# Attention over a masked graph on one core: 16 late key tiles instead of 12, their blocks moved by DMA alone and per query tile, and a new order on TensorE

## The reference, cut to what matters

```python
h = relu(layernorm(x))                         # x: 4096 x 256
adj = max(adjacency, eye)                      # 4096 x 4096
q, k, v = h @ Wq[hd], h @ Wk[hd], h @ Wv[hd]   # 8 heads, 64 wide
scores = q @ k.T * 64**-0.5 + 0.01*eye - 1e16*(1 - adj)
out = x + sum_hd(softmax(scores) @ v @ Wo[hd])
```

## Time and profile before

| | |
|---|---|
| three timed executions | 3120.87, 3127.58, 3130.91 us |
| profiled execution, span | 3131.2 us; no time of its own is listed apart from that span |
| granted TensorE clock, mean | 0.992 |
| TensorE busy | 3056.8 us (98%), 18368 matmuls |
| VectorE busy | 2444.3 us (78%) |
| ScalarE busy | 2171.6 us (69%) |
| GpSimd busy | 492.8 us (16%) |
| mean DMA rate | 86 GB/s |

### The profile page before, as it was taken

The page is one execution under the profiler, slowest core; times in us unless marked ns, Lnnn a source line. Parts: engine busy times, 40 slices in busy tenths (PEclk is TensorE's granted clock), DMA queues, the critical chain, the costliest instruction groups (busy, mean ns, idle before and its releaser), DMA issues.

```text
span 3131.2 us, 58791 instructions
## 1 busy us (share of the span) xinstructions
PE 3056.8 (98%) x18368; PEld 1892.8 (60%) x18368; DVE 2444.3 (78%) x4345; ACT 2171.6 (69%) x3297; POOL 492.8 (16%) x658
## 2 busy tenths in 40 slices
PE   7999999999999999999989999999999999999998
PEld 5566666666666666666556655666665666565664
DVE  6778788887878887887557877878877778777775
ACT  3677777777777777777547767767777667677675
POOL 3011111101111110111001111111111111111110
PEclk9999999999999999999999999999999999999999
DMA  5234444433444443344424433444433444433442
GB/s 154 53 85 88 95 79 98 84 81 78 91 91 84 94 85 85 73 95 87 94 74 80 88 84 73 87 93 81 93 79 72 86 94 81 93 79 72 89 93 52
DMA packets 217847, 267.82 MB, mean 86 GB/s; under 512 B 57472, under 2 KB 176768, under 8 KB 217728
## 3 DMA queue, kind: packets, MB, share of 16 engines
q1 hardware_dynamic: 173568, 178.51, 24.6%
q0 software_dynamic: 41984, 83.91, 16.1%
q10 hardware_dynamic: 2176, 4.19, 0.4%
HBM read 169.87 MB, written 12.71 MB: 58 GB/s over the span
## 4 chain that ended last, share of the span: by engine, by line
PE 92%; DVE 3%; issue 3%; DMA 1%; SPq 1%; DVEq 0%; ACT 0%; POOL 0%; POOLq 0%
PE psS L383 31%; PE psO L406 23%; PE psT L396 21%; PE psO L417 10%; PE psP L368 2%; PE psS L341 2%; DVE S L631 1%; PE psP L426 1%; PE psO L356 1%; PE psP L356 1%; DVE PT L645 1%; DMA S<-in_x 1%; SPq L239 0%; DMA S<-hT_scratch 0%; PE psT L327 0%
## 5 line engine op out<-in xcount | busy, mean ns | idle before, releaser
L631 DVE CUSTOM_DVE_ANT_0 S<-psS,B 128x1024 f32<-128x1024 f32 x1024 | 1239.6, 1211 | 169.0 <-PE psS L383 151.5
L517 ACT ACTIVATE S<-S,negm 128x1536 f32<-128x1536 f32 (+1 forms) x768 | 1094.8, 1427 | 62.9 <-DVE negm L638 59.7
L524 ACT ACTIVATE PT<-psT 128x512 f32<-128x512 f32 x768 | 457.0, 595 | 656.0 <-PE psT L396 654.3
L406 PE MATMUL psO<-PT,V 128*64 128x256 f32 x5120 | 836.0, 405 | 0.0
L396 PE MATMUL psT<-ident,S 128*128 128x128 f32 x5120 | 797.6, 283 | 31.4 <-DVE PT L645 24.3
L396 PEld LDWEIGHTS psT<-ident,S 128*128 128x128 f32 x5120 | 566.2, 141 | 398.2 <-issue 293.6
L383 PE MATMUL psS<-K,QH 128*128 128x512 f32 x2048 | 738.3, 442 | 8.4 <-DVE mx L631 5.9
L383 PE MATMUL psS<-K,QL 128*128 128x512 f32 x2048 | 643.8, 395 | 0.0
L645 DVE COPY PT<-psT 128x512 f32<-128x512 f32 x512 | 352.7, 689 | 332.4 <-PE psT L396 292.1
L658 DVE STREAM_TRANSPOSE S<-S 128x1536 f32<-128x1536 f32 x256 | 454.0, 1773 | 38.0 <-PE psO L417 37.9
L406 PEld LDWEIGHTS psO<-PT,V 128*64 128x64 f32 x5120 | 254.1, 135 | 362.4 <-issue 248.6
(11 more groups left out here) (52 smaller groups left out, 1056.1 us busy)
## 6 DMA issues: line engine op xcount, KB each, us to landing
S<-S SPq DMA_DIRECT2D x1536, 96.0 KB, 2.2
B<-in_adj POOLq DMA_DIRECT2D x256, 256.0 KB, 5.4
hq<-hT_scratch SPq DMA_DIRECT2D x32, 256.0 KB, 3.2
RB<-rden_scratch SPq DMA_DIRECT2D x128, 64.0 KB, 3.2
S<-in_x SPq DMA_DIRECT2D x8, 512.0 KB, 3.6
hT_scratch<-S ACTq DMA_DIRECT2D x8, 512.0 KB, 4.1
acc<-in_x POOLq DMA_DIRECT2D x16, 256.0 KB, 4.5
partial_scratch<-res POOLq DMA_DIRECT2D x16, 256.0 KB, 3.2
```

Of the source, the lines that this page charges most:

```text
L406: last = nc.tensor.matmul(psO[a * KD:(a + 1) * KD, 0:QW], V[:, 2 * s + a, h * KD:(h + 1) * KD], PT[:, s % RING, a * QW:(a + 1) * QW], star ...
L517: nc.scalar.activation(part, part, ACT.Exp, bias=negm[:, h % 2, q:q + 1], accum_out=sums[:, h % 2, q, e:e + 1]).then_inc(probs_ready, 1)
L524: nc.scalar.activation(PT[:, s % RING, :], psT[s % 2][:, :], ACT.Copy).then_inc(pt_act, 1)
L631: nc.vector.tensor_tensor_reduce(out=part, in0=psS[j % 2][:, :], in1=B[:, q, k * SLOT:(k + 1) * SLOT], scale=SCALE, scalar=LOWEST, op0=ALU ...
```

## The change

- `LATE` goes from 12 to 16, so TensorE transposes 16 key tiles in 8 slots instead of 20 in 10, and `values_late` has 16 tiles instead of 12. `T1` now covers the whole row of query tile 1 of the step before.
- All 16 pieces of a query tile are moved by DMA, one DMA for each piece and query tile, with a semaphore for each query tile: 32 DMAs a step on the SP queue instead of 12. `copy_late` is gone.
- ScalarE takes every transposed slot; VectorE's `take_slot` is gone.
- TensorE's step is four periods (`PERIODS`) of two transposed slots and two score slots; the late values stand in two halves, one in the third period and one behind the fourth, and slots 4 to 7 of the values at the end.
- On VectorE the order of the masks, of the sum of halves and of `add_heads` changes.

```diff
-LATE = 12
+LATE = 16
-MOVES = QUAD * (QUAD - 1)
+MOVES = QUAD * QUAD
...
-            sp.wait_ge(late_transposed, count(i, h, QT, QT))
-            for qi in range(QUAD):
-                for qj in range(QUAD):
-                    if qi != qj:
-                        src, dst = late_blocks(h, qi, qj)
-                        sp.dma_start(dst, src).then_inc(late_moved, 16)
+            for q in range(QT):
+                sp.wait_ge(late_transposed, count(i, h, QT, q + 1))
+                for qi in range(QUAD):
+                    for qj in range(QUAD):
+                        src, dst = late_blocks(h, q, qi, qj)
+                        sp.dma_start(dst, src).then_inc(late_moved[q], 16)
...
+        def values_late(i, h, tiles):
+            if tiles[0] == 0:
+                for q in range(QT):
+                    pe.wait_ge(late_moved[q], count(i, h, 16 * MOVES, 16 * MOVES))
...
+            for c in range(PERIODS):
+                for e in range(2):
+                    transposes(i, h, 2 * c + e)
+                    pair_scores(i, h, c, nxt, nxt2, e)
+                if c == 0 and nxt2 and h % 2 == 0:
+                    query(i2, h2, h2 == 0, isinstance(i, int) and i == 0 and h == 0)
+                if c == 1:
+                    values(i, h, 0)
+                    values(i, h, 1)
+                if c == 2:
+                    values(i, h, 2)
+                    values(i, h, 3)
+                    values_late(i, h, range(LATE_FIRST))
+                if c == 3 and prev and h % 2 == 0:
+                    if nxt2:
+                        pe.wait_ge(q_lo, count(i2, h2, 1, 2))
+                    project(*last_step(i, h))
+            values_late(i, h, range(LATE_FIRST, LATE))
+            for s in range(4, TS):
+                values(i, h, s)
...
+            if nxt:
+                mask(i1, h1, 6)
+                mask(i1, h1, 7)
+            if nxt2:
+                mask(i2, h2, 0)
+            if nxt:
+                transpose_late(i1, h1, 0, True)
+            if nxt2:
+                mask(i2, h2, 1)
+            if nxt:
+                transpose_late(i1, h1, 1, True)
```

More of the change, by code:

```diff
@@ L153, in wait_taken @@
     def wait_taken(engine, i, h, s):
-        slots, taken, start = (ACT_SLOTS, pt_act, PT_START) if s % TS in ACT_SLOTS else (DVE_SLOTS, pt_dve, 0)
-        engine.wait_ge(taken, count(i, h, len(slots), slots.index(s % TS) + 1 + start - (len(slots) if s < 0 else 0)))
+        engine.wait_ge(pt_act, count(i, h, TS, s + 1 + PT_START))
     def T1(h):
@@ L347, in keys_values @@
                 pe.wait_ge(wqo_in, 16 * (DC + 2))
-                query(0, 0, True, True)
+                query(0, 0, True, True, first=True)
             for u, read in ((0, v_act), (1, v_dve)):
@@ L358, in keys_values, with query @@
                 last.then_inc(v_proj, 1)
-        def query(i, h, wait_hq, first):
+        def query(i, h, wait_hq, free, first=False):
             if wait_hq:
@@ L427, in project, with pair_scores, step @@
             last.then_inc(projected, 2)
-        def step(i, h, nxt, nxt2, prev):
+        def pair_scores(i, h, c, nxt, nxt2, e):
             i1, h1 = (i, h + 1) if h + 1 < GROUP else (i + 1, 0)
             i2, h2 = (i, h + 2) if h + 2 < GROUP else (i + 1, h + 2 - GROUP)
-            for c in range(SUBSTEPS):
-                transposes(i, h, 2 * c)
+            j = 2 * c + 2 + e
+            if j < SLOTS:
                 if nxt:
-                    scores(i1, h1, c + 2)
-                if prev and h % 2 == 0 and c == PROJECT_AT:
-                    pe.wait_ge(q_lo, count(i, h, 1, 2))
-                    project(*last_step(i, h))
[L439 to L454, removed]
+                    scores(i1, h1, j)
+            elif nxt2:
+                scores(i2, h2, j - SLOTS)
+        def step(i, h, nxt, nxt2, prev):
+            i2, h2 = (i, h + 2) if h + 2 < GROUP else (i + 1, h + 2 - GROUP)
+            for c in range(PERIODS):
[14 more added lines that the diff above has]
+                        pe.wait_ge(q_lo, count(i2, h2, 1, 2))
+                    project(*last_step(i, h))
+            values_late(i, h, range(LATE_FIRST, LATE))
+            for s in range(4, TS):
+                values(i, h, s)
         pe.sem_inc(v_proj, START)
@@ L625, in mask @@
                 dve.wait_ge(bias_ready, i * QT + (q + 1))
-            if j == SPT + 1 and not first:
-                dve.wait_ge(late_moved, count(i, h, 16 * MOVES, 0))
-                dve.wait_ge(late_copied, count(i, h, QUAD, 0))
+            if not first:
+                for tq in range(QT):
+                    if j == t1_first_slot(tq):
+                        dve.wait_ge(late_moved[tq], count(i, h, 16 * MOVES, 0))
             wait_apart(dve, scores_ready, count(i, h, SLOTS, j + 1), dve_passed)
@@ L692, in step @@
             i2, h2 = (i, h + 2) if h + 2 < GROUP else (i + 1, h + 2 - GROUP)
[L693 to L700, removed]
-                    denominators(i, h)
-                if nxt2 and h % 2 == 0 and c > QUERY_AT:
-                    query_lo(i2, h2, c - QUERY_AT - 1)
-            if nxt:
-                mask(i1, h1, SLOTS - 2)
-                mask(i1, h1, SLOTS - 1)
-                transpose_late(i1, h1, 0, True)
+            if nxt:
+                mask(i1, h1, 2)
+                mask(i1, h1, 3)
+            if prev:
+                sum_halves(*last_step(i, h))
+            if nxt:
+                mask(i1, h1, 4)
+            if nxt2 and h % 2 == 0:
+                query_lo(i2, h2, 0)
+                query_lo(i2, h2, 1)
+            if nxt:
+                mask(i1, h1, 5)
+            denominators(i, h)
+            if h % 2 and not (isinstance(i, int) and i == 0 and h == 1):
+                add_heads(*((i, 1) if h == 3 else (i - 1, 3)))
+            if nxt:
+                mask(i1, h1, 6)
+                mask(i1, h1, 7)
             if nxt2:
```

91 lines of the change are left out of this document (42 added, 49 removed).

## The result

The changed kernel takes **4212.98 us** (median of 4 runs, 4207.15 to 4216.27), the kernel before 3127.8 us: a ratio of 1.347, 95% interval 1.345 to 1.349. The forecast was 3650 us in a range of 3010 to 4100: the direction was right, half of the slowdown was foreseen (522 us of 1085), and the measured time lies over the range's upper end.

The account below looks back on a forecast made before the run. The prediction took a ring through SP's 32 moves to bound the changed kernel: 10.3 + 16.5 = 26.8 us a step, 4.1 over before, 520 us more over 128 steps, so 3650 us. The range was 3010 to 4100 us.

Parts of the forecast that it names:

- the ring: Late values, TensorE's scores, mask, late transpose, SP's 32 moves, next late values: 10.3 + 31 c, 26.8 us a step.
- TensorE's own 20.2 us a step: TensorE's work in the new order, against 22.74 us; were that all, 325 us would be won.
- The issue interval c: Time from one late move's issue to the next on SP, taken as 0.53 us; break-even at 0.40.
- lower bound of 0.37: Lowest c on SP: denominators' store, 0.33 us, plus 0.04 between moves; gives a 21.8 us step and 3010 us.
- upper bound: Highest c on SP, about 0.64 us from the old two-row moves; gives a 30.3 us step and 4100 us.
- rival 2: SP's issue time doesn't change with the move's form: c 0.64 to 0.65, 4100 us; chance 0.27.
- three terms on TensorE: In the ring: late matmuls and change 1.89 us, transposed slot 0.41, score slot's start to its mask 1.38.
- busy share of about 75%: Expected sign in the profile after: TensorE's busy share falls from 98% to about 75%.
- The second ring: Not in the prediction: masks of slots 4 and 6 overwrite the block the moves read, so wait for the moves.
- VectorE and ScalarE at nothing: Both engines' changed work was costed at nothing while the step is longer than about 20 us.
- The landing: Last move's issue to landing, mean 2.7 us, plus 0.22 us for the semaphore to reach TensorE.
- The 50 ns: Skill's dispatch time for each DMA; with c near 0.1 the ring would be nowhere near TensorE.

Follow-up runs that it names:

- run 1: Changed kernel with half of the moves left out, 16 a step instead of 32, late probabilities wrong: 2811.14 us, ratio 0.899 to the kernel before.
- run 5: Changed kernel with the late transpose of query tile 0 ahead of the first mask of the step after next on VectorE: 4089.3 us, ratio 1.309.
- run 6: Changed kernel with the 16 moves of query tile 1 issued from ScalarE's queue, those of tile 0 from SP: 3654.87 us, ratio 1.168.
- run 4: Changed kernel with unread filler matmuls on TensorE, ten ahead of slot 6 and twelve ahead of the late values: 4130.51 us, ratio 1.320.
- run 2: Changed kernel with the first half of the late values moved from the third period to the end of the step: 4002.76 us, ratio 1.280.
- run 7: Kernel before with only its moves split by query tile, 24 one-row DMAs a step instead of 12 two-row ones: 3241.91 us, ratio 1.037.
- run 3: Changed kernel with both query tiles of a piece in one DMA, 16 two-row moves a step instead of 32: 4089.09 us, ratio 1.308.
- run 9: Changed kernel with 8 moves of a query tile by DMA, 4 pieces copied by ScalarE and 4 by GpSimd: 2938.63 us, ratio 0.940.

## Why the prediction was wrong in size

- **What bounds, and the ring.** Right. The chain of waits went from TensorE to SP's issues, and TensorE's late values wait for the moves once a step. Runs 1, 5 and 6 confirm it with numbers (1402 us for sixteen issues, 0.97 us for a 0.9 us earlier start, 558 us for a second queue).
- **TensorE's own 20.2 us a step.** Right as a floor: run 1 gained 317 us of the 325, with a step of 20.4 us. The step of before was read from one pair, 22.74 us; by the first move of each step over the whole trace it is 23.05, with 181 us outside the steps and not 220. The forecast total hardly feels it, since it adds the difference of steps to the whole.
- **The issue interval c. This is the step that failed first.** I took 0.53 from a single issue of the nearest form, the denominators' load. Measured: 0.63 from start to start (32 in 20.15 us), with 0.51 for the first move behind a pause, 0.59 in the median and 0.04 between. That is 3.2 us a step of the 4.6 that were missing (26.8 forecast, 31.4 measured), some 410 us. The trace of before had the warning. The same store of the denominators takes 0.33 us at 248.48, after a pause, but there is also this row of the same timeline of SP, right behind moves that end at 271.81:

```profile
271.86 0.58 SPq L241 DMA_DIRECT2D rden_scratch<-rden  x1
```

So the lower bound of 0.37 was none either. That row is no accident: in the trace of before seven stores begin within 0.1 us of the move ahead of them, 0.59 us in the median, and the 36 behind more than 1 us of pause take 0.33. For the store and for the move of one row an issue alone and an issue behind others are two prices (the move of two rows has 0.60 us for both); for 32 in a row only the second holds, and the twelve moves of before were the one row that showed it. That they stood as the upper bound (rival 2) gave 4100 us, 110 short.
- **The clock.** Not in the sum at all. All terms on TensorE were taken at full clock, though the prediction itself said that TensorE would wait 6 us a step. The three terms on TensorE are 1.5 us over the forecast ones in the mean of the turns (1.57 in the one shown); run 4 gets 0.64 us of a step back by filling part of the waits, so that much is shown for the clock by an experiment, and the rest by the granted clock beside the longer terms. This is what puts the time over the range: with c at its upper bound the sum was 30.3 us, and 31.4 were measured with an interval no longer than that bound. The busy share of about 75% came true (76%) by luck: the step is 4.6 us longer than forecast, and the matmuls are longer at the lower clock. Run 1 has the same matmuls busy for 2677.6 us, which would be 64% of this span.
- **The second ring.** Missed. I followed the semaphore of the moves to TensorE and not to the masks, which wait for it too, though the diff showed both. It didn't change this time much, since both rings have nearly the same length, but run 2 shows that it was decisive for any repair: the obvious one, late values at the end, gives 210 us instead of 800. The prediction also put all of TensorE's waiting at the late values; 3.5 us a step stand there, and 4.2 ahead of score slots, for masks.
- **VectorE and ScalarE at nothing.** Right: 53% and 44% busy.
- **The landing.** 2.7 us and 0.2 to reach TensorE: near enough in the mean (3.08 us from the last move's start to the late values, 2.9 forecast). It varies from 2.1 to 6.0 us.
- **The 50 ns that the prediction cites.** The Trainium skill, page "DMA: Bandwidth & Descriptors", section "Anatomy of one DMA — SWDGE (gpsimd) path", has about 50 ns of dispatch and a small, variable time for the descriptors. That section is on DMAs issued by GpSimd, and the moves here are issued by SP and ScalarE, so it was no measure for them: they take 0.51 to 0.61 us an issue, in every form tried. By the same page's section "Rules for kernel authors" DMAs spread over several engines only save the issuing engine's time. Run 6 agrees on what is saved, and here just that was worth 558 us.

## What to carry to other kernels

Count a DMA queue like an engine: number of issues by the interval between issues back to back, read from a row in which several follow each other, never from a lone one. Then follow each semaphore of the changed part to all who wait for it, and for each look whether what it does leads back to the next issue; a queue that is half idle on the average sets the pace as soon as it lies in such a ring. And a sum that makes TensorE wait some microseconds has to price what it does next at the lower clock.

## What the runs showed of the hardware that was not expected

- One issue on SP takes 0.59 to 0.60 us whether it carries one row of 2048 bytes a partition, one of 1536 or two of 2048 (medians 591 ns in the changed kernel, 591 in run 7, 599 in run 3). Behind a pause the move of one row takes 0.51, the move of two rows 0.60 as well (kernel before and run 3).
- Two queues issuing at once barely slow each other in the median (592 and 612 ns).
- A wait of 3.6 us on TensorE costs behind it: sixteen late matmuls and the change took 2.66 us instead of 1.8 to 1.9, with the granted clock at 0.69 over that stretch.
- GpSimd and ScalarE copy 32 partitions of 512 float32 elements in the time of one DMA issue, 0.62 and 0.63 us (run 9).
